# One 8-head attention pass of a four-layer graph network: two GpSimd multiplications given to VectorE

## What is computed

```python
msg = (x @ W_s + b_s)[senders]            # 8 heads of 32 columns
r = (x @ W_r + b_r)[receivers]
logits = einsum('ehk,k->eh', leaky_relu(msg + r), a_w) + a_b
e = exp(logits - segment_max(logits, receivers)[receivers])
agg = segment_sum(e / segment_sum(e)[receivers] * msg, receivers)
```

## Time and profile before

| what | value |
| --- | --- |
| median of 3 runs | 5627.22 us (5620.43 to 5628.62) |
| the profiled execution's own time | 5618.88 us |
| span of its profile | 5616.8 us |
| pass 3, roughly | 1950 to 2790 us |
| pass 4, roughly | 2790 to 3700 us |
| busy share of the span | PE 77%, PEld 58%, DVE 66%, ACT 55%, POOL 57% |

### The profile page before, as it was taken

The page is one execution under the profiler, slowest core; times in us unless marked ns, Lnnn a source line. Parts: engine busy times, 40 slices in busy tenths (PEclk is TensorE's granted clock), DMA queues, the critical chain, the costliest instruction groups (busy, mean ns, idle before and its releaser), DMA issues. The chain is left out here.

```text
span 5616.8 us, 80182 instructions
## 1 busy us (share of the span) xinstructions
PE 4348.7 (77%) x20170; PEld 3260.2 (58%) x20170; DVE 3708.2 (66%) x10668; ACT 3066.9 (55%) x8955; POOL 3225.3 (57%) x2882
## 2 busy tenths in 40 slices
PE   0344339899999799989688888869999997777675
PEld 0111116567777477777566777657878874554453
DVE  8522213445777476666478778757778778888886
ACT  0133225555899656555355555535555556766666
POOL 2577777762676545455356456534444347777774
PEclk9655559999999899999899889869999997877777
DMA  1478644443666556556445555535544434444441
GB/s 40 152 256 260 221 130 154 146 151 108 193 206 199 195 177 210 179 198 210 150 147 186 166 177 184 172 108 161 165 147 160 147 122 133 131 133 135 143 136 61
DMA packets 360222, 905.84 MB, mean 161 GB/s; under 512 B 69943, under 2 KB 144159, under 8 KB 359770
## 3 DMA queue, kind: packets, MB, share of 16 engines
q1 hardware_dynamic: 249578, 626.47, 32.9%
q0 software_dynamic: 110192, 274.25, 16.3%
HBM read 565.74 MB, written 340.13 MB: 161 GB/s over the span
## 5 line engine op out<-in xcount | busy, mean ns | idle before, releaser
L1067 PE MATMUL psum<-got,sf 128*128 128x256 f32 x1600 | 628.4, 481 | 441.5 <-ACT got L1325 399.8
L2320 POOL DMA_INDIRECT got<-tab,end_i x600 | 703.6, 1173 | 458.2 <-PE psum L1176 285.8
L2320 POOL DMA_INDIRECT got<-hop,end_i x600 | 643.7, 1073 | 434.7 <-PE psum L1067 201.6
L1067 PEld LDWEIGHTS psum<-got,sf 128*128 128x128 f32 x1600 | 322.8, 227 | 723.1 <-DMA got<-in_x,src_i 288.5
L1176 PE MATMUL psum<-got,sf 128*128 128x264 f32 (+2 forms) x1200 | 412.5, 430 | 250.3 <-DVE got L2045 201.0
L1971 DVE TENSOR_TENSOR res<-psum,own 128x512 f32<-128x512 f32 x300 | 206.3, 688 | 449.1 <-DMA own<-in_x,own_i 240.6
L1325 ACT COPY got<-psum 1x256 f32<-1x256 f32 x796 | 282.1, 354 | 401.0 <-PE psum L1067 274.0
L1176 PEld LDWEIGHTS psum<-got,sf 128*128 128x128 f32 x1200 | 225.5, 220 | 355.4 <-DVE got L2045 263.0
L1311 ACT CAST sf<-s 128x512 f32<-128x512 uint8 x350 | 214.4, 613 | 347.7 <-DVE s L1960 215.2
L1363 ACT ACTIVATE res<-res,l_mo 128x256 f32<-128x256 f32 x600 | 310.9, 589 | 140.7 <-DVE l_mo L1934 140.5
L1215 ACT ACTIVATE squares<-res,l_sv 128x256 f32<-128x256 f32 x600 | 297.3, 497 | 165.2 <-DVE l_sv L1946 106.8
(11 more groups left out here) (511 smaller groups left out, 12855.7 us busy)
## 6 DMA issues: line engine op xcount, KB each, us to landing
own<-hop SPq DMA_DIRECT2D x150, 512.0 KB
x_t<-res SPq DMA_DIRECT2D x150, 512.0 KB
xo<-x_t SPq DMA_DIRECT2D x150, 512.0 KB
hop<-res SPq DMA_DIRECT2D x100, 512.0 KB
tab<-tab SPq DMA_DIRECT2D x50, 536.0 KB
own<-tab SPq DMA_DIRECT2D x50, 536.0 KB
r_t<-rec_b SPq DMA_DIRECT2D x50, 528.0 KB, 3.7
rec_b<-r_t SPq DMA_DIRECT2D x50, 528.0 KB, 4.1
```

The costliest lines, as they stand in the source:

```text
L1067: T.matmul(o, sf_of(q)[:, k * P:(k + 1) * P], got_of(q)[:, k * FEAT:(k + 1) * FEAT], start=(p < 3), stop=True).then_inc(at("l_agg"), 1)
L2320: eng.indirect_dma_start(out=dst, out_offset=None, in_=table, in_offset=bass.IndirectOffsetOnAxis(ap=idx, axis=0), bounds_check=rows_ - 1, ...
```

## The change

`ew` is no longer a piece of POOL: its multiplication is a third instruction of VectorE's `ez`, and `es` comes after `ez` itself. `mine` of pass 4 is VectorE's, with the copy of the weights first and the multiplication second. The planner gets 3.6 us for `ez` in place of 2.4, and 1.35 us for `mine` on VectorE in place of 2.9 on POOL, and writes a new order for all engines with these.

```diff
@@ schedule
-                put(("V", "ez", q), 2.4, here("Vr0", "Vr1", "Stab0", "Stab1", "Vx1b"))
-                put(("G", "ew", q), 2.6, here("Vez"))
-                put(("V", "es", q), 1.42, here("Gew"))
+                put(("V", "ez", q), 3.6, here("Vr0", "Vr1", "Stab0", "Stab1", "Vx1b"))
+                put(("V", "es", q), 1.42, here("Vez"))
...
-                me = "Gmine" if p == HOPS else "Vmine"
-                put((me[0], "mine", q), {4: 2.9, 5: 0.62, 6: 1.15}[p], here("Sexp", "Yown"))
+                me = "Vmine"
+                put(("V", "mine", q), {4: 1.35, 5: 0.62, 6: 1.15}[p], here("Sexp", "Yown"))
@@ vector_link, "ez"
                 V.scalar_tensor_tensor(zf, zf, 0.01, zf, ALU.mult, ALU.max).then_inc(at("l_ez"), 1)
+                eng.wait_ge(at("l_ez"), i + 1)
+                zh = zf.rearrange("p (m c) -> p m c", c=cols1)
+                V.tensor_tensor(zh, zh, over(aw[:], K * heads1), ALU.mult).then_inc(at("l_ew"), 1)
@@ vector_gat
+            elif name == "mine" and p == HOPS:
+                eng.wait_ge(at("g_p"), j + 1)
+                eng.wait_ge(*own_landed(q))
+                c4, weight = split_heads(own_f, g), by(pp[:, par, 1, 0:hk])
+                V.tensor_copy(own_f[:, :, g.flat:g.ext], weight)
+                V.tensor_tensor(c4, c4, weight.unsqueeze(3).to_broadcast([P, K, g.heads, g.cols]), ALU.mult).then_inc(at("g_w"), 1)
@@ gpsimd_link
-            elif name == "ew":
-                eng.wait_ge(at("l_ez"), i + 1)
-                zh = z_of(q).rearrange("p (m c) -> p m c", c=cols1)
-                G.tensor_tensor(zh, zh, over(aw[:], K * heads1), ALU.mult).then_inc(at("l_ew"), 1)
-            elif name == "mine":
-                eng.wait_ge(at("g_p"), i + 1)
-                eng.wait_ge(*own_landed(q))
-                own_f = by_chunk(own_of(q), g1.width)
-                c4, weight = split_heads(own_f, g1), pp[:, par, 1, 0:K * heads1].rearrange("p (k h) -> p k h", k=K)
-                G.tensor_tensor(c4, c4, weight.unsqueeze(3).to_broadcast([P, K, heads1, cols1]), ALU.mult)
-                G.tensor_copy(own_f[:, :, g1.flat:g1.ext], weight).then_inc(at("g_w"), 1)
```

## The result

The changed kernel takes 5721.45 us (median of 4 runs) beside 5623.83 us (median of the three runs shown above and one more): a ratio of 1.0175 (95% interval 1.016 to 1.0191), some 98 us slower. The forecast had the sign, at 5655; the time lies above the range. The profiled execution's span is 5712.5 us, 95.7 us longer than before.

What follows compares the result with a forecast made beforehand. PE was taken as nearest its limit in passes 3 and 4 (88% and 85%), idling behind DVE's order. Terms 27 + 10 - 1 = +36 us on 5618.9 gave 5655; range 5585 to 5705 for 8 in 10, likeliest case 5639 to 5690.

Steps and rivals of the forecast that it cites:

- What bounds pass 3: Pass 3: `sh` stands behind the previous group's `ez`, so about every second group loses PE some 2 us.
- The term for `ew`: Pass 3: one more multiplication in front of late `sh`, 22 x 1.23 = 27 us; bounds -44 and +59.
- the bound: Pass 3: `es` straight behind `ez` makes a late `sh` come 2.7 us later, 22 x 2.7 = 59 us.
- The sign that would show it: Pass 3 some 25 us longer, PE's wait of line 971 from 44 to 70 us, `sh` 3.5 to 5 us behind `rs`.
- The rival "faster": Pass 3: the new order takes `sh` ahead of `ez`, up to -44 us, giving 5584 or 5606; chance 0.29.
- The rival "absorbed": Pass 3: DVE's added 61 us lie under PE's work, PE idles no more than now, giving 5628; chance 0.18.
- `mine`: Pass 4: weighting in front of `lead`, net of the ended shut-out, +10 us; bounds -48 and 70.
- The lock and the gathers: POOL's indirect DMAs would lose up to 100 x 0.65 = 65 us to DVE's 100 added instructions.

Runs made afterwards that it cites:

- e6: Every engine in the order of the kernel before; VectorE does the row multiplication inside `ez`, the weighting stays on GpSimd: 1.0071 of the kernel before.
- e9: As e6, with the sum over the heads and the bias (`es`) in the same block behind `ez` too: 1.0167 of the kernel before.
- e13: Order of the kernel before, row multiplication on VectorE; block of `ez`, multiplication and `es` in even groups only, late multiplication in the others: 1.0135 of the kernel before.
- e14: As e13, but with the block in the odd groups only: 1.003 of the kernel before.
- e2: The change with only the row multiplication on VectorE, planned anew; pass 4's weighting stays on GpSimd: 1.0148 of the kernel before.
- e4: The new order of e2, with the row multiplication left out altogether, on VectorE and GpSimd: 1.0101 of the kernel before.
- e5: The change with the row multiplication as its own piece, it and `es` ranked 2.5 groups later in the planner: 1.0008 of the kernel before.
- e1: The change with only pass 4's weighting on VectorE, planned anew; the row multiplication stays on GpSimd: 1.003 of the kernel before.
- e7: Both parts on VectorE, every engine in the order of the kernel before; row multiplication at the head of `es`, `mine` right behind `vals`: 0.9961 of the kernel before.
- e12: The same kernel as e7, run again with more rounds: 0.9953 of the kernel before.
- e3: Order of the kernel before; VectorE does only the row multiplication, at the head of `es`, with the weighting left on GpSimd: 0.9982 of the kernel before.
- e8: The kernel before, order unchanged, without GpSimd's multiplication of the own rows in pass 4; VectorE gets nothing: 0.9955 of the kernel before.
- e10: As e1, but the planner must put the weighting behind `lead`: 1.0005 of the kernel before.
- e11: As e1, but the planner is told 0.2 us for the weighting in place of 1.35: 1.0058 of the kernel before.

## Why the prediction was right and wrong

**What bounds pass 3: right.** It named PE's late transposes behind `sh`, and `sh` behind `ez`. e6 and e9 put one multiplication, and then the sum with its bias too, in that place: `sh` came 1.26 and 2.80 us later and PE's wait rose by 1.26 and 3.34 us in the groups shown. The 0.54 us more in e9 are PE's own: there its wait begins 0.96 us after the leaky relu does, and 1.50 before.

**The term for `ew`: the step that failed.** The prediction saw that the planner's rule puts `es` straight behind `ez`, and gave 59 us for it, but took one operation, "27 us", as if `es` stayed where it was. In the order that was built, `es` follows the multiplication at once in all 50 groups.

Both prices were short besides, because they counted PE's waits alone and gave its clock nothing. One operation costs 40 us in the old order (e6), not 27, and 33 of them show as a longer pass 3 in its profile. PE's wait for the transposes rises by 65.7 - 44.0 = 22 us, about as priced, but of the 33 us 15 are busy time for the same 3272 matmuls, at a granted clock of 0.94 in place of 0.96 (e6's wait, 1990 to 2790 us, and its pass 3):

```profile
PE psum L971 <- ACT res L1363: 65.7, 20, 6.8
```

```profile
1962.00:2808.00 846.00, 738.95 (x3272) 604.78 (x3270) 574.59 (x1204) 464.36 (x1148) 271.78 (x231) 0.94 0.51 179
```

The block in the even groups costs 76 us (e13), not 59. Here too the wait rises by just the 59 us that were priced, 103.0 - 44.0, and PE's busy time in pass 3 by some 30 beside it, at 0.92:

```profile
1962.00:2859.00 897.00, 753.93 (x3291) 616.04 (x3289) 580.51 (x1205) 466.01 (x1151) 260.13 (x233) 0.92 0.49 169
```

Of the odd groups the prediction said that `x1a` moves "some 2 us", and put no price on that: 17 us (e14). Together the block is 93 us where the sum had 27 and the bound 59. The lower clock needs no new sequence: with that of PE unchanged, e9's pass 3 has the same granted clock as the change's, 0.92:

```profile
1962.00:2875.00 913.00, 752.52 (x3285) 613.18 (x3283) 583.71 (x1204) 462.62 (x1149) 251.53 (x231) 0.92 0.48 166
```

**The sign that would show it: half wrong.** It named a rise of PE's wait of line 971 to 70 us. That is what e6 and e9 do in the old order; in the change's own order that wait halved, and PE waits for `x1a` behind the block instead. The new order loses about as much, +82 us (e2) beside e9's +100 in pass 3's landmark, but at other places of PE: beside the wait for `x1a`, 42 us more go to ScalarE's copies, which the prediction didn't name. What makes these waits stays open (e4 and e5).

**The rival "faster": refuted.** `sh` did come ahead of more `ez`: it stands right behind the block in 8 groups, where it stood behind `ez` in 20, and the waits for the transposes fell to 22.2 us. It didn't help. `x1a` stands there in 26 groups as before, but behind 5.3 us in place of 2.4. That POOL is spared was worth nothing: its gathers waited for their ring all the more. The rival "absorbed" fails by e6: PE has nothing ready there.

**`mine`: the size right, in part by luck: two effects that it didn't part nearly cancel.** +10 was forecast, e1 measured 0.3% (17 us), and the landmarks of pass 4 +8 to +11. DVE's weighting lines grew by 138.5 - 129.8 = 8.7 us, where +10 was costed; that DVE as a whole would be busy for 10 us more was wrong, as it was busy for 15 less. But in the old order the same work makes pass 4 8 to 17 us shorter (e7, e12). So the new order of pass 4 costs about 20 us. In the old order both parts on VectorE gain 22 to 26 us, and the row alone 10 (e3): there the weighting is a gain in itself, and the end of the shut-out, with POOL spared (25 us in e8), pays for more than the added work. Which place in pass 4's order costs these 20 us is open: e10 and e11 moved one entry each and told nothing apart.

**The lock and the gathers.** The estimate that POOL's indirect DMAs would lose up to 65 us to DVE's added work didn't show: a gather took 1.20 us in the mean of pass 3 before and 1.14 after, here in the groups of POOL after:

```profile
L2328 POOL DMA_INDIRECT got<-hop,end_i x172 | 196.5, 1142 | 417.5 <-PE psum L1066 376.0 <-issue 41.2 <-ACT res L1362 0.3
```

The exclusive lock that the Trainium skill describes (SBUF — State Buffer, section "SBUF: two separate sides") is borne out by e8, where taking GpSimd's operation away brought the copy from 1.10 us to 0.18.

## What to carry to other kernels

Work that goes from a side engine to a busy one is priced by what stands behind its new place in the queue, not by its length: the same 61 us of VectorE cost nothing behind the short instruction that feeds the critical chain (e3), and 40 us in front of it (e6). A piece whose input used to come from another engine loses a natural gap as well when it moves; ask what the scheduler will now put directly behind it, and price that whole block, with the clock that PE loses behind longer waits. If two engines shut each other out, count the disturbed durations on both before saying that moving work to one of them adds to its load.

## What the runs showed of the hardware

PE's busy time is no constant of its work. Pass 3 has the same 3272 to 3274 matmuls before and after and is busy 724 and 758 us, at a granted clock of 0.96 and 0.92 of full speed (a mean over its two levels, 1.2 and 2.4 GHz). PE idled longer in it, 139 us in place of 89, so some 34 of the 84 us lost are counted as busy. Single stretches show the lower level behind the longer waits. In the earlier trace rows PE idles for 1.96 us and then works at the full clock (the first line below). In the change it works at the full clock, idles for 3.10 us behind the block, and is then at half of it for the next 6 us:

```profile
2508.68:2512.00 3.32, 3.13 (x18) 2.53 (x19) 2.35 (x4) 2.45 (x6) 1.21 (x2) 1.00 0.61 185
```

```profile
2654.00:2659.00 5.00, 4.01 (x17) 2.57 (x15) 4.17 (x7) 2.69 (x10) 0.00 (x0) 1.00 0.62 211
2662.10:2664.00 1.90, 1.89 (x4) 1.15 (x4) 0.78 (x3) 1.06 (x1) 1.29 (x3) 0.50 0.95 319
2664.00:2668.00 4.00, 3.55 (x9) 2.38 (x8) 3.59 (x13) 0.72 (x2) 2.03 (x2) 0.50 0.41 129
```

So a delay in front of PE can cost more than its own length. No run varied the wait alone, so what share of the lost clock is due to the waits isn't shown.
